# Routed experts: from every expert on every row to 128-row blocks of chosen rows, with the order of all steps read from a table

## What is computed

```python
logits = x @ W_router.T                       # 8 experts
probs  = softmax(logits); rw, sel = top_k(probs, 2)
combine = zeros((T, 8)).at[arange(T)[:, None], sel].add(rw)
sh = (silu(gate) * up of x @ Ws_gate_up) @ Ws_down        # shared, hidden 704
shared_out = sh * sigmoid(x @ W_sgate.T)
gu = einsum('th,ehi->eti', x, We_gate_up)                 # every expert, hidden 176
h  = silu(gu[..., :176]) * gu[..., 176:]
sparse_out = einsum('eth,te->th', einsum('eti,eih->eth', h, We_down), combine)
out = layernorm(x + shared_out + sparse_out)
```

## Time and profile before

| what | us |
|---|---|
| median of 3 runs | 464.75 (464.39 to 466.61) |
| the profiled execution, its own time | 466.61 |
| its span, first to last instruction | 464.9 |
| mean granted TensorE clock, share of full speed | 0.911 |

### The profile page before, as it was taken

One profiled execution on the slowest core, in us unless ns is written; L12 is line 12 of the kernel. 1 busy time (PEld: TensorE's weight loads), 2 busy tenths in 40 slices (PEclk: granted clock), 3 DMA queues, 4 the chain that ended last, 5 costly groups with the idle time before them and its releaser, 6 DMA issues.

```text
span 464.9 us, 7904 instructions
## 1 busy us (share of the span) xinstructions
PE 394.7 (85%) x3034; PEld 243.1 (52%) x3034; DVE 295.4 (64%) x656; ACT 204.4 (44%) x386; POOL 110.2 (24%) x150
## 2 busy tenths in 40 slices
PE   0958987777789877887997869999899999999996
PEld 0435656534546422233474335656446777777675
DVE  4483357976774993356469975734557968656754
ACT  4576446556126404696762044335563323222421
POOL 2345455445331001565200011012220000000000
PEclk9977889889959865899998579999999999999999
DMA  7940000133000000122000000000000000000001
GB/s 227 368 146 1 1 1 2 45 92 89 3 1 2 0 1 0 57 88 62 1 1 0 1 1 1 2 0 1 1 2 0 1 13 2 11 24 2 1 13 34
DMA packets 6856, 15.14 MB, mean 33 GB/s; under 512 B 738, under 2 KB 4130, under 8 KB 6818
## 3 DMA queue, kind: packets, MB, share of 16 engines
q1 hardware_dynamic: 6820, 14.65, 9.8%
HBM read 13.60 MB, written 1.05 MB: 32 GB/s over the span
## 4 chain that ended last, share of the span: by engine, by line
PE 58%; DVE 22%; ACT 9%; issue 6%; POOL 4%; DMA 1%; POOLq 0%; DVEq 0%
PE psum_a L640 24%; PE psum_b L640 10%; DVE arena_mixers L1290 8%; PE psum_a L776 5%; PE psum_b L848 3%; ACT arena_mixers L1050 2%; PE psum_a L838 2%; PE psum_a L880 1%; DVE arena_ffn L1332 1%; PE psum_b L830 1%; PE psum_a L875 1%; PE psum_a L647 1%; PE psum_b L788 1%; PE psum_b L760 1%; DVE arena_ffn L1329 1%
## 5 line engine op out<-in xcount | busy, mean ns | idle before, releaser
L640 PE MATMUL psum_a<-cut_weights,x_transposed 128*128 128x352 f16 (+3 forms) x774 | 134.9, 327 | 13.3 <-DVE cut_weights L1115 11.9
L640 PEld LDWEIGHTS psum_a<-cut_weights,x_transposed 128*128 128x128 f16 x774 | 75.1, 101 | 62.6 <-DVE cut_weights L1115 12.5
L1406 POOL TENSOR_TENSOR ln_rstd<-ln_var_eps,minus_half 128x1 f32<-128x1 f32 x32 | 19.7, 615 | 196.6 <-DVE ln_var_eps L1106 196.6
L1065 ACT ACTIVATE arena_ffn<-psum_a 128x352 f32<-128x352 f32 x48 | 22.3, 465 | 86.8 <-PE psum_a L640 86.8
L1423 POOL TENSOR_SCALAR_AFFINE_SELECT arena_mixers<-arena_mixers 128x256 f32<-128x256 f32 (+1 forms) x48 | 25.2, 529 | 98.0 <-ACT arena_mixers L1050 97.9
L1290 DVE TENSOR_REDUCE arena_mixers<-psum_a 128x2 f16<-128x768 f32 (+3 forms) x44 | 47.0, 1127 | 2.1 <-PE psum_a L822 2.1
L640 PE MATMUL psum_b<-cut_weights,arena_ffn 128*128 128x256 f16 (+1 forms) x408 | 46.7, 273 | 0.0
L1050 ACT ACTIVATE arena_mixers<-psum_a 128x1024 f32<-128x1024 f32 (+2 forms) x48 | 41.7, 880 | 8.0 <-PE psum_b L640 4.1
L640 PEld LDWEIGHTS psum_b<-cut_weights,arena_ffn 128*128 128x128 f16 (+1 forms) x408 | 39.1, 98 | 6.8 <-issue 1.7
L1329 DVE SCALAR_TENSOR_TENSOR arena_ffn<-arena_ffn,psum_a 128x352 f32<-128x352 f32 x48 | 24.9, 519 | 25.7 <-ACT arena_ffn L1065 14.4
L1332 DVE SCALAR_TENSOR_TENSOR arena_ffn<-arena_ffn,router,psum_a 128x176 f32<-128x176 f32 (+1 forms) x80 | 31.9, 433 | 1.7
(11 more groups left out here) (171 smaller groups left out, 640.4 us busy)
## 6 DMA issues: line engine op xcount, KB each, us to landing
stage<-in_wup SPq DMA_DIRECT2D x8, 512.0 KB, 3.6
stage<-in_wdown SPq DMA_DIRECT2D x4, 512.0 KB, 4.1
arena_ffn<-in_w SPq DMA_DIRECT2D x1, 1408.0 KB, 7.2
stage<-in_xT SPq DMA_DIRECT2D x2, 512.0 KB, 4.2
stage<-in_wqkvg SPq DMA_DIRECT2D x2, 512.0 KB, 5.2
residual<-in_x SPq DMA_DIRECT2D x2, 512.0 KB, 7.4
out<-residual SPq DMA_DIRECT2D x8, 128.0 KB, 1.7
stage<-in_wqkv SPq DMA_DIRECT2D x2, 384.0 KB, 9.0
```

Of the source, the lines that this page charges most:

```text
L640: ins = mm(dst, lhs[k][a], rhs(k, b, col), start=(k == 0 and a == 0 and b == 0), stop=(bias_at is None and k == n - 1 and a == 1))
L1065: nc.scalar.activation(TG[:, n % 2, :], ps[:, 0, 0:MCW], ACT.Tanh, scale=0.5 * UN).then_inc(mu_tanh, 1)
L1406: g_.tensor_tensor(rstd[:, r:r + 1], veps[:, r:r + 1], half[:, 0:1], ALU.pow).then_inc(ln_rstd[layer], 1)
```

## The change

The last part computes only the chosen experts, per batch.

- `rt` and `rc` also make, for each tile, the two 0/1 rows of the picks (`pick`, `picks16`) and running sums over the batch's tiles (`before16`), and write four words behind each row of `X` (row number, second expert, weight, difference of the weights), so that rows of `X` are now 260 words long.
- `rk` (new): two 8-column products count the earlier rows with the same expert; DVE turns the count into two row numbers of a buffer in device memory. `sx` (new): two indirect transfers per tile on POOL's queue scatter the 128 rows to them (`expert_in`).
- `rb` (new, once per batch): 13 small DVE instructions make the table of the batch's 15 blocks: for each block its expert and the row it starts at.
- For each of 2 x 15 blocks: SP loads a row number into a register and reads 128 rows from there (`XB`); `bx`: two transposes; `bu`: PE loads the offset of the block's expert into a register, 6 products of 352 columns with weights at that offset; `bt`: two transposes; `bd`: 6 products of 256 columns, scaled by the row's weight on ACT (`OB`), and an indirect transfer on POOL's queue scatters the rows to `expert_out`. `bi`: 8 small DVE instructions per 5 blocks for the targets and weights.
- The shared part is apart: `su`, 12 times: 12 products of 512 columns for 128 hidden units, tanh on ACT, two DVE instructions; `sh`: head on ACT, rest on POOL; `sd`, 8 times: 18 products of 256 columns.
- `os`: when all blocks of a batch are back, SP reads each tile's two results (`OL`), POOL adds them; `fin`: DVE adds the row and the norm follows as before.
- At the start SP fills `expert_in` (9,984 rows of 1,040 bytes) from a small constant, between the 8th and the 9th piece of weights.
- 23 pieces in place of 21; the last four overwrite the weights of layer 0 and of `qk`, so they wait for the last `qk`.
- The planner is gone. `ORDER` lists 598 steps and the PSUM place of each.

```diff
-HID = NE * FE + FS
+BB = TB * 2 + NE - 1
+NBLK = NB * BB
+ROW = D + 4
+SLOTS = NE * TB + NE - 1
+DEEP = 3
+GROUP = 5
...
+            load(7)
+            sp.dma_start(expert_in.rearrange("(j p) d -> p j d", p=P), row_init.unsqueeze(1).to_broadcast([P, NB * SLOTS, ROW])).then_inc(rows_clear, 16)
+            for i in range(8, len(PIECES)):
                 load(i)
+            for g, (a, e) in enumerate(GROUPS):
+                b = a // BB
+                if a % BB == 0:
+                    for t in range(b * TB, b * TB + TB):
+                        sp.wait_ge(sent[t], 32)
+                    sp.wait_ge(tabled, 2 * b + 1)
...
+                for j in range(a, e):
+                    row = sp.value_load(blk_r[0:1, j:j + 1], min_val=0, max_val=(NB * SLOTS - 1) * P)
+                    sp.dma_start(XB[:, j % (2 * GROUP), :], expert_in[bass.ds(row, P), :]).then_inc(blocks_in[g], 16)
+            sp.wait_ge(pe_done, PLACE[("ya", NB - 1, TB - 1)][3])
+            for b in range(NB):
+                for i in range(4):
+                    sp.wait_ge(returned[i], 16 * len(range(i, BB * (b + 1), 4)))
+                for t in range(b * TB, b * TB + TB):
+                    for k in range(2):
+                        first = (k * NT + t) * P
+                        sp.dma_start(OL[:, t, k, :], expert_out[first:first + P, :]).then_inc(outs_in[t], 16)
...
+                elif kind == "bu":
+                    j = step[1]
...
+                    offset[j] = pe.value_load(blk_u[0:1, j:j + 1], min_val=0, max_val=(NE - 1) * REC)
+                    pe.wait_ge(xb_rest, j + 1)
+                    claim(step)
+                    for k in range(KD):
+                        for a, c in ((0, 0), (0, 1), (1, 0)):
+                            ins = mm(ps[:, 0:2 * FE], XBT[:, j % DEEP, a, k, :], ws[:, c, bass.ds(offset[j] + k * 2 * FE, 2 * FE)],
+                                     start=(k == 0 and a == 0 and c == 0), stop=(k == KD - 1 and a == 1))
...
+                elif kind == "sx":
+                    t = step[1]
+                    pool.wait_ge(placed, t + 1)
+                    if t == 0:
+                        pool.wait_ge(rows_clear, 16)
+                    for k in range(2):
+                        g_.indirect_dma_start(expert_in[:, :], bass.IndirectOffsetOnAxis(ap=place_u[:, 2 * t + k:2 * t + k + 1], axis=0),
+                                              X[:, t, :], None).then_inc(sent[t], 16)
+                elif kind == "bd":
+                    j = step[1]
+                    pool.wait_ge(blk_out, j + 1)
+                    g_.indirect_dma_start(expert_out[:, :], bass.IndirectOffsetOnAxis(ap=blk_to[:, j:j + 1], axis=0),
+                                          OB[:, j % 4, :], None).then_inc(returned[j % 4], 16)
```

More of the change, by code:

```diff
@@ L17 @@
 NE, FE, FS = 8, 176, 704
-HID = NE * FE + FS
-MC, MCW = 6, 352
-HK = (HID + P - 1) // P
+BB = TB * 2 + NE - 1
[4 more added lines that the diff above has]
+GROUP = 5
+GROUPS = [(a, a + GROUP) for a in range(0, NBLK, GROUP)]
+REC = KD * 2 * FE + 2 * D
 LAST = F0 % P
@@ L179, in dependences @@
             add(("cen", i), at(i > 1, ("cen", 1)))
[L180 removed]
+        add(("split", i), at(i, ("split", i - 1)), at(i in (1, 2), ("cen", i)), ("qk", NB - 1, TB - 1) if name == "wexp" and first < EARLY else None)
     add(("bias", 0), ("cen", 2))
@@ L209, in dependences @@
         add(("wo", 2, t), ("ty", t), at(t > 1, ("ln", 2, t - 2)))
-    for layer, of in enumerate(("wo", "dn", "wo", "md")):
+    for layer, of in enumerate(("wo", "dn", "wo", "fin")):
         for t in range(NT):
@@ L272, in schedule @@
 def schedule():
     need = dependences()
-    after = {step: [] for step in need}
-    last_of_kind = {}
+    waiting = {}
     for step in need:
-        key = step[:2] if step[0] in ("ln", "tx", "wo") else step[0]
-        if key in last_of_kind:
-            need[step].append(last_of_kind[key])
-        last_of_kind[key] = step
-        for x in need[step]:
-            after[x].append(step)
-    ordered = {}
-    while len(ordered) < len(need):
-        ordered.update({step: True for step in need if step not in ordered and all(x in ordered for x in need[step])})
@@ L289, in schedule @@
-    span = {}
-    for step in reversed(ordered):
-        span[step] = sum(w for _, w in engine_times(step)) + max((span[x] for x in after[step]), default=0)
-    order = []
-    free = dict.fromkeys("TADP", 0.0)
-    tiles = {("A", i): [i - 9, 0.0] for i in range(RING_A)}
-    tiles.update({("B", i): [i - 9, 0.0] for i in range(RING_B)})
-    kept = None
-    end, tile_of = {}, {}
-    landed = [4.1 + 1.6 * i + (1.5 if i > 2 else 0) for i in range(5)]
-    left = {step: len(x) for step, x in need.items()}
@@ new lines, in schedule @@
+        key = f"{step[0]}{step[1]}" if step[0] in ("ln", "tx", "wo") else step[0]
+        waiting.setdefault(key, []).append(step)
+    order, tile_of = {}, {}
+    for word in ORDER.split():
+        key, _, tile = word.partition(":")
+        step = waiting[key].pop(0)
+        assert all(x in order for x in need[step]), step
+        order[step] = True
+        if tile:
+            tile_of[step] = (tile[0].upper(), int(tile[1]))
+        elif step[0] == "pv":
+            tile_of[step] = tile_of[(*step[:3], 0)]
@@ L342, in schedule @@
     assert len(order) == len(need)
-    return order, tile_of
+    return list(order), tile_of
 RING_A, RING_B = 3, 2
```

605 lines of the change are left out of this document (391 added, 214 removed), and 54 rows, old and new, of tables (COST, NUDGE).

## The result

The changed kernel takes 471.54 us (median of 4 runs, 471.24 to 476.95) against 464.75. The ratio is given with its interval as 1.0165, 95% 1.0088 to 1.0243 (the quotient of the two medians is 1.0146). So it is some 1.5% slower where 2.5% faster was forecast; the time lies inside the range of 434 to 483. The profiled execution has a span of 469.7 us, 16.7 more than the forecast 453.0.

A forecast was written before the change was run, and what follows sets the result against it. The prediction took PE's work to bound the last part: 272 us before it, 159 for it (135.1 / 0.85), 4.5 for register loads and 17.5 of tail gave a 453.0 us span, so 453 forecast; range 434 to 483.

The forecast's parts named there:

- what PE gains, 108.2 us: Last part: PE work added by shared products, block products, transposes and counts, 108.2 us, against 146.4 us removed.
- the 135.1 of the sum: Last part: PE's remaining work of 143.1 us less 8.0 for batch 1's `sd`, taken as off the path.
- the third rival: Behind the last router: blocks do not fill PE and its clock falls, 84 us in place of 67, total 470; chance 0.12.
- Share of PE: Last part: PE busy 0.85 of the time, the share of 177 to 235 us before, giving 159 us.
- Registers: PE's offset load before each block's `bu`: 0.15 us uncovered for each of 30 loads, 4.5 us.
- the rival's condition: Register loads holding PE's queue in full at each `bu`: equal to the old time at 0.55 us per block; chance 0.17.
- Cover of batch 1's dispatch: Last router to batch 1's first block: some 12 to 15 us covered by other steps, 0 counted; 12 without cover.
- Tail: After the last `bd`: scale, scatter, reads, sums, four norms and the write take 17.5 us, against 4.55 before.
- Start of the last part: The last part was taken to begin at 272 us, as before; earlier stages keep their work, only its order changes.
- PE is fed as well as now: Last part: PE share 0.965 and register loads covered, 427 us total; chance 0.10 for 427 to 441.
- the late fill: Layer 0: filling `expert_in` delays the 9th weight piece, at most 17 us of stall, up to 470; chance 0.08.
- POOL as the bound: Last part: indirect transfers of 3.5 us or more give POOL 200 us, total 475 and above; chance 0.05.

The follow-up runs named there:

- e2: Changed kernel without the product of the rows' head with the weights' rest in `bu` and `bd`: 467.9 us over all six runs.
- e1: Changed kernel with PE's expert offsets fixed in the program in place of register loads: 462.1 us, ratio 0.9974 to the kernel before.
- e11: Changed kernel with SP reading every block from the constant row table, without register load or wait for scatters and table: 468.5 us, 1.0084 to the kernel before.
- e3: Changed kernel without the product with the row's rest in the blocks and the two DVE instructions making the rests: 466.9 us, 1.0041 to the kernel before.
- e14: Changed kernel with constant PE offsets, blocks read from the constant table without waits, and no weight-rest products in blocks: 460.1 us, 0.987 to the kernel before.
- e4: Changed kernel with batch 1's results not read back, rows of x read in their place without waiting for the last scatters: 474.2 us, 1.0218 to the kernel before.
- e6: Changed kernel, full computation, with PE loading the next block's offset right behind the current `bu` products: 469.3 us, 1.0063 to the kernel before.
- e8: Changed kernel with 10 blocks per batch in place of 15, the last five left out with all their steps: 459.7 us, 0.9853 to the kernel before.
- e10: Changed kernel with two of three float16 products in `su`, the one with the row's rest dropped: 471.2 us, 1.0123 to the kernel before.
- e7: Changed kernel with constant PE offsets and batch 1's results not read back: 470.4 us, 1.0127 to the kernel before.
- e12: Changed kernel, full computation, with a batch's 15 PE register loads together ahead of its first block's transposes: 482.4 us, 1.037 to the kernel before.
- e13: Changed kernel with constant PE offsets and blocks read from the constant row table without waits or SP register loads: 461.6 us, 0.9921 to the kernel before.

## Why the prediction was wrong

**The step that failed is what PE gains, 108.2 us, and with it the 135.1 of the sum.** Measured are 152.3 at a share of 0.837. With that work, the measured start and the measured tail, the forecast's own formula gives 268 + 152.3 / 0.85 + 4.5 + 19.7 = 471.4, against 469.7. Of the 17.2 some 15 can be placed:

- *Pace, some 8 us.* `bd` was priced at the 0.111 of a run of 51 products; it takes 0.143, 0.19 more per block, 5.7 in all; a pair of transposes takes some 0.03 more than two of a run, 1.8 with both pairs of each block; the four `sd` 2.16 each from start to start and not 2.0, 0.6. `bu` and `su` were right.
- *Clock, some 7 us.* 0.93 over 72 us and 0.89 over 47 mean (0.07 x 72 + 0.11 x 47) x 2 = 20 us at the lower level. PE was busy 18.4 us of them, twice as long as its work takes at full clock, so 9.2 us were added; before had 3.9 us of this, all busy, 2.0. This was the third rival, at 0.12, and it came in part, in another place: 0.95 was to separate it, and it is 0.93 and 0.89 behind the maxima, but the stretch behind the last router that the rival named (374 to 450) has 1.00. The Trainium skill, page "TensorE: Matmul & The Clock Gate", section "Part 1: The HAM clock gate", says that an idle PE is set back to half clock; the trace agrees at the wait of 2.35 us with 10.2 us at half speed behind it, while in `e2` waits of 0.75 us at most have as long a fall behind them. `e1` and `e11` got 5.2 and 3.2 us through this one stretch.

The last 2 us or so are not placed. How much each part cost in time, and not in PE's work, is not shown by its size, as the next step says.

**Share of PE: the value right, the meaning wrong.** 0.85 was forecast, 0.837 measured, but "what is taken from PE there is taken from the path" does not hold any more. Taking 15.7 us away gave 6.4 in `e3`, and nothing clear in `e14`; adding 13 cost 6.9. The share moves with the work left out (0.83 in the changed kernel's stretch, 0.79 in `e3`, 0.81 in `e14`), so it is not a constant by which work can be divided, and that 0.85 came out nearly right beside a wrong sum of work is luck. `e14` argues that with less PE work the chain would still have taken nearly as long. Leaving the clock and the two waits aside, which of the hops sets the chain stays open.

**Registers: the term right, the rival half.** 0.15 uncovered per load was taken and 0.15 is measured in 375 to 450 us; 4.5 stands. All 30 loads together are worth 8.9 (0.30 each), of which 5.2 came by way of one longer wait and the clock behind it, so the rival's condition (0.55 per block) did not hold. The Trainium skill's page "DMA: Bandwidth & Descriptors", section "Latency and other measured facts", gives a floor of about 600 ns for the load; here it took 302 ns at the median and 648 at the longest, and the measurement decides.

**Cover of batch 1's dispatch: 0 taken, 1.8 us measured** at the first block, out of the 12 without cover, and 5.5 in all with the stretch at the lower clock.

**Tail: 17.5 taken, 19.7 measured**, with POOL's scatter cheaper (0.96). The first `fin` comes 7.8 us behind the last `bd`, 1.0 more than its terms (6.75); the four tiles take 8.4 us (457.77 to 466.13), as forecast; and the last write takes 3.6 and not 2.1. That the `sd` leave the path was right only in the sense that the rows' way back takes as long; `e4` shows that they then bind by themselves.

**Start of the last part: 272 taken, 268 measured, by luck.** 2.6 of these 4 us are there already at the last row-maxima product (265.4 against 268.0), which moves between 264.2 and 271.6 in kernels with the same instructions up to it. That the fill did not hold ACT up (0 taken) was near: it landed 1.3 us before ACT's cut of that piece. "PE is fed as well as now", the late fill and POOL as the bound did not occur. DVE (308.6 against 313) and ACT (221.7 against 227) were sized rightly.

No version tried with the full computation beats the old kernel; `e6` comes nearest, at 1.0063 [1.0022, 1.0104]. 26.6 us of PE's total is gone, and none of it is time. From the start of the last part to PE's last product there (the last `bd`, with the four `sd` now behind it) PE works 29.1 us less than before (181.35 to 152.3), but it stands idle for 29.7 us in place of 6.7, and the tail behind is 14.8 us longer, counted from 460 before and from 450 now. With the start 4 us earlier that makes the 4.8 us of span by which the change loses: -29.1 + 23.0 + 14.8 - 4.

## What to carry over

A share of an engine read from a stage prices only work that keeps that stage's run lengths: price short runs by short runs (two transposes, six products), and where none is there, take the pace of the shortest. When many small dependent steps replace long runs, ask first what each hop and each wait costs, and leave room for PE's clock, which here stayed at its lower level for 3.4 to 10.2 us behind such waits. Before comparing variants by their medians, count from an instruction ahead of the first difference: here the same instructions arrived up to 7 us apart. Then look for two variants that share a stretch unchanged: what differs there (2.5 us here) is what one profile can't tell.

## What the runs showed that was not expected

- The stage from 30 to 137 us, the same instructions in all variants, has a granted clock of 0.76 (`e8`, `e10`) to 0.84 (`e1`), and the maxima end at 264.2 to 271.6 by it. What decides it was not found.
- At 355.7 to 358.4 DVE and ACT both wait, the one for an `sd` that PE's row has ending at 355.7, the other for a `bu` ending at 356.7, and both go on at 358.44. POOL issues four indirect transfers in a row there (352.61 to 357.44). In `e1` the same wait of DVE is 1.11 us. It is no chance: PE's wait behind it is 2.35, 2.34 and 2.35 us in the three kernels that are the changed one up to there, and 0.9 to 1.1 in `e1`, `e6`, `e7`, `e11`, `e12` and `e13`, in which PE's or SP's register loads stand elsewhere or are gone. Its cause was not tried.
- The clock's fall does not go by that wait alone: in `e2`, PE's longest waits there are 0.69 and 0.75 us, and the lower level still lasts 10.2 us (365.2 to 375.4); in `e12` 1.07 us has no fall behind it.
- Leaving out products can leave PE's busy time where it was (55.41 and 55.57 us with 14 fewer in `e14`), because the clock falls.
